# Causal attention between two expert layers: all scores of a head pair in one run, per-head work of exp, cast and low part merged, routing moved into the context bank

## What is computed

```
x = x + 0.5 * ffn(layernorm(x))      # 8 experts, the best one per token
x = x + attn(layernorm(x))
x = x + 0.5 * ffn(layernorm(x))
attn: q, k, v = tanh(x @ W + b)      # 16 heads of 64, per batch row of 512 tokens
      p = softmax(causal(q k^T / 8)); ctx = p v;  tanh(ctx @ Wo + bo)
ffn:  logits = x @ gate; e = argmax; first 320 tokens of an expert are kept
      relu(x @ w1[e] + b1) @ w2[e] + b2, times the probability of e
```

## Time and profile before

| | us |
|---|---|
| median of 3 runs | 523.68 (523.2 to 523.76) |
| profiled execution | 527.28 |
| its span, first to last instruction | 525.5 |
| TensorE busy | 434.2 (83%) |
| VectorE busy | 304.7 (58%) |
| ScalarE busy | 254.5 (48%) |
| POOL busy | 255.6 (49%) |
| mean granted TensorE clock | 0.929 of full |

### The profile page before, as it was taken

The page is one execution under the profiler, slowest core; times in us unless marked ns, Lnnn a source line. Parts: engine busy times, 40 slices in busy tenths (PEclk is TensorE's granted clock), DMA queues, the critical chain, the costliest instruction groups (busy, mean ns, idle before and its releaser), DMA issues.

```text
span 525.5 us, 11791 instructions
## 1 busy us (share of the span) xinstructions
PE 434.2 (83%) x4395; PEld 294.2 (56%) x4395; DVE 304.7 (58%) x926; ACT 254.5 (48%) x441; POOL 255.6 (49%) x277
## 2 busy tenths in 40 slices
PE   1742999528799999999999999899999788499960
PEld 1611687404566766566576566566666543167850
DVE  6781344638977767378856488774698713222213
ACT  1100433106587888487757577775777511034310
POOL 6471154712765565265455556456556440205550
PEclk9995899958899999999989999999999887789995
DMA  8812343163000000000000000000000000125315
GB/s 269 288 53 53 95 152 100 51 221 128 1 2 1 2 2 2 0 2 2 1 2 1 23 2 1 3 1 11 13 1 2 2 20 1 45 73 161 123 54 167
DMA packets 31515, 28.06 MB, mean 53 GB/s; under 512 B 2732, under 2 KB 27365, under 8 KB 31208
## 3 DMA queue, kind: packets, MB, share of 16 engines
q1 hardware_dynamic: 27184, 19.97, 12.7%
q0 software_dynamic: 2560, 4.74, 2.8%
q10 hardware_dynamic: 1720, 2.66, 1.4%
HBM read 16.84 MB, written 10.52 MB: 52 GB/s over the span
## 4 chain that ended last, share of the span: by engine, by line
PE 61%; DVE 12%; POOL 10%; issue 9%; DMA 5%; ACT 1%; SPq 0%; DVEq 0%; POOLq 0%; ACTq 0%
PE sc L710 12%; PE sc L589 7%; PE pj L599 7%; PE pj L680 5%; PE tT L747 4%; PE cx L730 3%; PE cx L732 3%; PE sc L715 3%; PE pj L690 3%; DVE Ph L1073 3%; POOL disp L332 3%; PE cx L731 3%; PE tT L551 3%; DMA ytok<-empty 3%; POOL Pl L360 2%
## 5 line engine op out<-in xcount | busy, mean ns | idle before, releaser
L360 POOL TENSOR_TENSOR Pl<-Pf,Ph 128x512 f16<-128x512 f32 (+1 forms) x64 | 61.9, 982 | 74.6 <-DVE Ph L1073 74.6
L710 PE MATMUL sc<-Tq,Tk 64*128 64x128 f32 (+3 forms) x512 | 95.5, 471 | 0.0
L360 POOL TENSOR_TENSOR Pl<-Wf,Ph 128x512 f16<-128x512 f32 (+1 forms) x64 | 58.6, 931 | 49.2 <-DVE Ph L1073 49.2
L343 POOL DMA_INDIRECT ytok<-Y,who x48 | 49.5, 1031 | 67.8 <-DVE Y L941 56.7
L1073 DVE CAST Ph<-Pf 128x512 f16<-128x512 f32 (+1 forms) x96 | 55.2, 607 | 41.6 <-ACT Pf L494 40.9
L730 PE MATMUL cx<-Vh,Ph 128*128 128x65 f16 x640 | 66.7, 197 | 14.1 <-POOL Vl L360 10.6
L434 ACT ACTIVATE hT<-sc,RT 128x320 f32<-128x320 f32 x64 | 33.8, 528 | 91.2 <-PE sc L589 90.3
L730 PEld LDWEIGHTS cx<-Vh,Ph 128*128 128x128 f16 x640 | 59.8, 99 | 16.4 <-POOL Vl L360 12.0
L731 PE MATMUL cx<-Vl,Ph 128*128 128x64 f16 x640 | 66.7, 195 | 0.0
L732 PE MATMUL cx<-Vh,Pl 128*128 128x65 f16 x640 | 66.5, 195 | 0.0
L1073 DVE CAST Ph<-Wf 128x512 f16<-128x512 f32 (+1 forms) x96 | 53.8, 591 | 20.0 <-ACT Wf L494 19.6
(11 more groups left out here) (181 smaller groups left out, 876.3 us busy)
## 6 DMA issues: line engine op xcount, KB each, us to landing
W<-in_L_ffn_w SPq DMA_DIRECT2D x32, 256.0 KB
disp<-empty SPq DMA_DIRECT2D x2, 1290.0 KB, 7.4
XE<-disp SPq DMA_DIRECT2D x16, 129.0 KB
ytok<-empty SPq DMA_DIRECT2D x2, 1024.0 KB, 12.6
G<-ytok SPq DMA_DIRECT2D x8, 256.0 KB, 3.8
out<-X SPq DMA_DIRECT2D x4, 256.0 KB, 2.3
ytok<-Y,who POOLq DMA_INDIRECT x48
XE<-disp SPq DMA_DIRECT2D x16, 32.2 KB
```

The lines of the kernel that those rows point to most:

```text
L343: pool.indirect_dma_start(ytok[phase], bass.IndirectOffsetOnAxis(ap=who[u][0:m, j:j + 1], axis=0), Y[u][0:m, j, :], None).then_inc(y_sc[u] ...
L360: pool.tensor_tensor(dst, src, hi, ALU.subtract).then_inc(done, 1)
L710: mm(score_bank(h, c)[:, o:o + w], Tk[u][half(h), P * kt:P * kt + P], Tq[u][half(h), P * kt:GN], start=kt == kts[0], stop=False)
```

## The change

- The two heads of a pair share tiles: Pf, Ph and Pl become [128, 2, 1280], and one exp, one cast and one low cover both heads of a chunk.
- TensorE does all scores of a pair in one run, then all masks, then the context of head 0. Chunk 2 of both heads goes to halves of bank pj1; the second half waits until the first is written (`half_ps`). Chunk c of head h is in sc[2c + h] otherwise.
- K is projected ahead of Q, and waits in pj1 for the exp of chunk 2 of the pair before. Tanh of K comes ahead of tanh of Q.
- ScalarE casts V (`v_high`) ahead of the exps, and all three exps come ahead of tanh of V.
- POOL does the low of V first, then one low of chunk 0 for both heads. VectorE does the lows of chunks 1 and 2, each behind its cast.
- A context waits for all lows of its pair at head 0.
- Routing goes into bank cx, in step 7 (logits) and in step 0 of the batch after (ranks), each right behind the projections and behind a wait for normalise of head 1 of pair i - 3. `choose` stays in step 7, `place` is now ahead of the first cast of step 0.
- The last output projection uses pj0.

```diff
-ORDER = [(c, h) for c in range(3) for h in range(2)]
-POOL_LOWS = [(0, 0), (0, 1), (2, 0), (2, 1)]
-V_LOWS = [(1, 0), (1, 1)]
+SCORED = [(c, h) for c in range(3) for h in range(2)]
+SCORES_IN = (2, 4, 6)
...
+        Pf0, Ph0 = sb("Pf0", [P, 2, 1280], F32), sb("Ph0", [P, 2, 1280], F16)
+        Pf = [Pf0, Wf[:, 0:2560].rearrange("p (h n) -> p h n", h=2)]
+        Ph = [Ph0, sb("Ph1", [P, 2, 1280], F16)]
+        Pl = [sb(f"Pl{u}", [P, 2, 1280], F16) for u in range(2)]
...
-        sc = [bank(f"sc{i}") for i in range(4)]
+        SC = ctx.enter_context(nc.psum_tensor("sc", [P, 4, 512], F32))
+        sc = [SC[:, i, :] for i in range(4)]
...
+        def scored(s, u, c):
+            a, n, _ = CHUNKS[c]
+            source = pj1[:].rearrange("p (h n) -> p h n", h=2) if c == 2 else SC[:, 2 * c:2 * c + 2, :]
+            return slice(a, a + n), source, 6 * s + SCORES_IN[c]
 
         def score_bank(h, c):
-            return sc[2 * h + (c == 1)]
+            return pj1[:, 256 * h:256 * h + 256] if c == 2 else sc[2 * c + h]
...
             def p_low(s, u):
-                for c, h in POOL_LOWS:
-                    a, n, _ = CHUNKS[c]
-                    pool.wait_ge(S["p_hi"], 6 * s + 2 * c + h + 1)
-                    low(Pl[u][h][:, a:a + n], Pf[u][h][:, a:a + n], Ph[u][h][:, a:a + n], S["p_lo_p"])
+                pool.wait_ge(S["p_hi"], 3 * s + 1)
+                low(Pl[u][:, :, 0:GN], Pf[u][:, :, 0:GN], Ph[u][:, :, 0:GN], S["p_lo_p"])
...
                 if score:
+                    v_low(i - 1, 1 - u)
                     p_low(i - 1, 1 - u)
-                    v_low(i - 1, 1 - u)
...
             def exps(s, u, c):
-                a, n, _ = CHUNKS[c]
-                for h in range(2):
-                    act.wait_ge(S["s_ps"], 6 * s + 2 * c + h + 1)
-                    if not (isinstance(s, int) and s < 2):
-                        act.wait_ge(*low_part(s - 2, h, c))
-                    act.activation(Pf[u][h][:, a:a + n], score_bank(h, c)[:, 0:n], ACT.Exp, scale=0.125,
-                                   bias=pshift[:]).then_inc(S["exp_done"], 1)
+                at, source, ready = scored(s, u, c)
+                act.wait_ge(S["s_ps"], ready)
+                if s >= 2:
+                    act.wait_ge(*((S["p_lo_v"], 2 * (s - 2) + c) if c else (S["p_lo_p"], s - 1)))
+                act.activation(Pf[u][:, :, at], source, ACT.Exp, scale=0.125, bias=pshift[:]).then_inc(S["exp_done"], 1)
...
                 if score:
-                    exps(i - 1, 1 - u, 0)
-                    exps(i - 1, 1 - u, 1)
+                    v_high(i - 1, 1 - u)
+                    for c in range(3):
+                        exps(i - 1, 1 - u, c)
                 if project:
                     tanh_v(i, u)
-                if score:
-                    exps(i - 1, 1 - u, 2)
                 if turn:
                     copy_ct(i - 3, (r - 3) % NPAIR)
-                if score:
-                    v_high(i - 1, 1 - u)
...
-                if not first:
-                    pe.wait_ge(S["tv"], i)
-                for w, ps, done in ((0, pj0, "q_ps"), (1, pj1, "k_ps")):
-                    if w and not first:
-                        pe.wait_ge(S["tk"], i)
-                    if w and r == 0 and not first:
-                        pe.wait_ge(S["rank_read"], NS + b - 1)
+                for w, ps, done in ((1, pj1, "k_ps"), (0, pj0, "q_ps")):
+                    if w and i == 1:
+                        pe.wait_ge(S["tk"], 1)
+                    if w and i >= 2:
+                        pe.wait_ge(S["exp_done"], 3 * (i - 2) + 3)
+                    if not w and i:
+                        pe.wait_ge(S["tv"], i)
...
+            def scores(s, u, project):
+                if s:
+                    pe.wait_ge(S["exp_done"], 3 * s)
+                pe.wait_ge(S["tq"], s + 1)
+                pe.wait_ge(S["tk"], s + 1)
+                def part(h, c, kt):
+                    o, q = KOFF[kt] - CHUNKS[c][0], P * kt
+                    return mm(score_bank(h, c)[:, o:o + GN - q], Tk[u][half(h), q:q + P], Tq[u][half(h), q:GN],
+                              start=(c, kt) in ((0, 0), (1, 1)) or (c, h) == (2, 0), stop=False)
                 for h in range(2):
+                    part(h, 0, 0)
+                for h in range(2):
+                    part(h, 1, 1)
+                for h in range(2):
+                    part(h, 1, 3)
+                if project:
+                    pe.wait_ge(S["tk"], s + 2)
+                part(0, 2, 2).then_inc(S["half_ps"], 1)
+                pe.wait_ge(S["half_ps"], s + 1)
+                part(1, 2, 2)
+                for c, h in SCORED:
...
             def context(c, u, h):
                 if h == 0:
                     pe.wait_ge(S["v_lo"], c + 1)
-                pe.wait_ge(S["p_hi"], 6 * c + h + 5)
-                pe.wait_ge(*low_part(c, h, 2))
-                pe.wait_ge(*low_part(c, h, 1))
-                if h or not (isinstance(c, int) and c == 0):
+                    pe.wait_ge(S["p_lo_p"], c + 1)
+                    pe.wait_ge(S["p_lo_v"], 2 * c + 2)
+                if c or h:
                     pe.wait_ge(S["ctxn"], 2 * c + h)
...
                 if project:
-                    qk(i, b, r)
+                    kq(i, b, r)
+                if route:
+                    pe.wait_ge(S["ctxn"], 2 * (i - 3) + 2)
+                    route()
                 if early:
                     if turn:
                         tt_free(i - 3)
                     early()
                 if score:
-                    scores(i - 1, 1 - u, 0)
-                    scores(i - 1, 1 - u, 1, c1_read)
+                    scores(i - 1, 1 - u, project)
                 if mix:
+                    if cx_read:
+                        pe.wait_ge(*cx_read)
                     context(i - 2, u, 0)
                 if project:
                     v(i, b, r)
-                if score:
-                    scores(i - 1, 1 - u, 2)
...
-                late = {7: lambda: rank_batch(b - 1, pj1)}
-                end = {6: lambda: route_logits(b - 1, sc[1])}
-                c1_read = {7: (S["dl_ready"], NS + b)}
+                route, cx_read = {7: lambda: route_logits(b - 1, cx)}, {7: (S["dl_ready"], NS + b)}
+                if b > 1:
+                    route[0], cx_read[0] = lambda: rank_batch(b - 2, cx), (S["rank_read"], NS + b - 1)
...
+            step(NG, 0, project=False, route=lambda: rank_batch(NG - 2, cx), cx_read=(S["rank_read"], NS + NG - 1))
...
+            def p_high(s, u, c):
+                at = scored(s, u, c)[0]
+                dve.wait_ge(S["exp_done"], 3 * s + c + 1)
+                if s >= 2:
+                    dve.wait_ge(S["ctx_ps"], 2 * (s - 2) + 2)
+                dve.tensor_copy(Ph[u][:, :, at], Pf[u][:, :, at]).then_inc(S["p_hi"], 1)
...
                 if score:
-                    split_high(i - 1, 1 - u, 0)
+                    p_high(i - 1, 1 - u, 0)
                 if mix:
                     normalise(i - 2, u, 0)
                 if score:
-                    split_high(i - 1, 1 - u, 1)
-                if late:
-                    late()
-                if score:
-                    split_low(i - 1, 1 - u)
-                    split_high(i - 1, 1 - u, 2)
+                    for c in (1, 2):
+                        p_high(i - 1, 1 - u, c)
+                        p_low(i - 1, 1 - u, c)
...
-                    step(b, r, between={4: lambda: add_out(b - 1), 5: lambda: norm_batch(b, b - 1),
-                                        7: lambda: choose(s, NS + b - 1, 0, GT, sc[1])}.get(r),
-                         late=(lambda: batch_place(b - 1, s, pj1)) if r == 7 else None)
+                    between = {4: lambda: add_out(b - 1), 5: lambda: norm_batch(b, b - 1),
+                               7: lambda: choose(s, NS + b - 1, 0, GT, cx)}
+                    if b > 1:
+                        between[0] = lambda: batch_place(b - 2, s, cx)
+                    step(b, r, between=between.get(r))
...
+            step(NG, 0, between=lambda: batch_place(NG - 2, s, cx))

```

More of the change, by code:

```diff
@@ L507, in step @@
                 if project:
-                    tanh_qk(i, r)
+                    tanh_kq(i, r)
                 if between:
@@ L692, in v @@
                 last.then_inc(S["v_ps"], 1)
-            def scores(s, u, c, bank_read=None):
-                first = isinstance(s, int) and s == 0
-                if c == 0:
-                    pe.wait_ge(S["tq"], s + 1)
-                    pe.wait_ge(S["tk"], s + 1)
-                if c == 2:
-                    pe.wait_ge(S["exp_done"], 6 * s + 2)
-                elif not first:
-                    pe.wait_ge(S["exp_done"], 6 * (s - 1) + (6 if c == 0 else 4))
-                if bank_read:
-                    pe.wait_ge(*bank_read)
-                a, n, kts = CHUNKS[c]
-                for kt in kts:
-                    o, w = KOFF[kt] - a, GN - P * kt
-                    for h in range(2):
```

(24 more changed lines are left out.)

67 lines of the change are left out of this document (21 added, 46 removed).

## The result

| | us |
|---|---|
| median before | 523.72 (523.2 to 525.42, 4 runs) |
| median after | 560.62 (558.53 to 564.24, 4 runs) |
| ratio | 1.0707 (1.0665 to 1.0749) |
| profiled execution after (before) | 558.53 (527.28) |

A forecast was written before the change was run, and what follows sets the result against it. TensorE's own list was taken to bound plain steps, with stalls for VectorE's lows elsewhere. Step terms of +23.2 and +4.5 for the clock gave +27.7 on 523.68: 551.4 us, range 531 to 562.

The forecast's parts named there:

- The plain step: Attention step without routing or rescaling: would grow from 7.98 to 8.3 us, +0.35 with roundings, in 28 steps.
- TensorE's list: TensorE's own work in a plain step: -0.62 for masks, +0.43 and +0.31 for chunk 2, sum +0.12 us.
- a passage: TensorE's switch from 128 rows to 64 and back around masks: costs 0.31 us, one in place of three.
- Rival 3: Merged cast over two heads loses its fast form and takes 1.226, +0.5 us a plain step: 565 us; chance 0.04.
- The chain on VectorE: Cast of chunk 1 waits for POOL's low (2.15); late normalise makes TensorE wait 2.6 us at logits and ranks.
- Rival 1: POOL's long instruction doesn't hold VectorE's cast, normalise ends 1.5 us earlier: 539.4, or 533 without plain stall; chance 0.22.
- Step 5: Rescaling step: later pow and normalise raise the second context's stall from 0.5 to 2.9 us; step some 10.9.
- steps 4 to 6: These steps of each batch together: +1.8 us, three times 5.4.
- The merged exps: ScalarE's merged exps save 3 x 0.2 us of its time, costed at nothing because ScalarE is busy 48%.
- First four steps, bound by VectorE: Start of the attention: VectorE gains lows and a v_low collision, loses some collisions; +1 us (-1 to +3).
- The clock: Granted clock halves behind long stalls: three more falls of 1.5 us for five new stalls, +4.5 (0 to +9).
- steps 7 and 0: Routing steps, logits then ranks: 23.0 us together against 19.6 and 18.1, +3.4 and +4.9, with 2.6 waits.

The follow-up runs named there:

- Experiment 3: The changed kernel with chunk 2 of the first head issued right behind chunk 0, chunk 2 of the second behind its own chunk 1: 542.33 us (ratio 1.0369).
- experiment 4: The changed kernel with the masks of each chunk right behind its scores again: 545.0 us (ratio 1.0411).
- experiment 2: The changed kernel with POOL's one low of 1024 columns as two of 512, one for each head: 559.58 us (ratio 1.067).
- Experiment 10: The changed kernel with one exp for each head again, six in place of three, casts and lows left merged: 565.14 us (ratio 1.0789).
- experiment 5: The changed kernel with normalise of the first head ahead of the cast of chunk 0 on VectorE: 568.69 us (ratio 1.0864).
- experiment 6: The changed kernel with POOL's low of V behind its low of chunk 0 again: 566.21 us (ratio 1.0805).

## Why the prediction was right, and where it was off

**The plain step** (8.3, measured 8.26) is right in each term: TensorE's list +0.13 for +0.12, the wait of the second context 0.15 for 0.2. Experiment 3 shows that the losses it named are the heads sharing a bank and the wait between the halves, and experiment 4 the 0.31 of a passage. Rival 3 is out: the merged cast took 0.69 (196.31), and the merged exp 1.11.

**The chain on VectorE** was forecast as POOL's low 2.15 (2.14), the cast behind it, normalise at T + 7.15 (7.18), and a wait for cx of 2.6 (2.64, 2.63, 2.64). Rival 1 rested on a cast that isn't held. The rule behind the forecast, that a cast ends just behind POOL's instruction, came from one row, and it held; on so thin a base that was in part luck. The Trainium skill (SBUF — State Buffer, Who interferes with whom) says that a VectorE instruction in a 2-port mode, or one with two SBUF inputs beside a GpSimd instruction that reads SBUF, contends with GpSimd, and that the first to issue keeps the shared interfaces for its whole length. The runs agree for both kinds: a cast of 2.23, subtractions of 2.06, 2.02 and 3.03. For this chain the forecast used only the first kind (the second only for a small product in step 5). By the second, splitting POOL's low hands the wait to the subtraction behind the cast, as experiment 2 shows.

**Step 5** (10.9) measured 10.95 in batches 2 and 3 and 11.32 in batch 1. In batch 2 it grew by 2.46. The waits of over 0.1 ahead of its two contexts grew by 2.14 (2.04 + 0.46, against 0.36 before); the rest is near the plain step's 0.28. The forecast had 2.4 for the stall. Its sum for steps 4 to 6 (+1.8, measured 1.75 in batches 2 and 3) leaves out the plain step's 0.35 in one of the three steps, and a stall taken somewhat too long makes up for that.

**"The merged exps ... I cost that at nothing"** has no effect on the sum, because the plain stall was computed with the exp of 1.11, but as a price it is wrong. Experiment 10 measured 0.15 a plain step. ScalarE's share (48% before) says nothing about it: the first exp lies on the path masks, exp, cast, normalise, second context. The forecast had written that path down and then judged the merge by the share.

**"First four steps, bound by VectorE: +1 (-1 to +3)"** is the term that failed, at +5.0 in the profiled execution. Three things were left out. Projection of K into pj1 waits for the exp of chunk 2 of the pair before, and in step 2, with no contexts yet to cover it, that is the 1.56 at 133.64. The second context's wait for normalise, which in a plain step is 0.15, stands here behind the rescaling and a product of 128x4 elements that met the low of V and took 1.07 in place of 0.16 (4.32, where TensorE had waited 2.85 before, for the low of V). And the granted clock was 0.50 behind it, in 145.30 to 147.00, and already in 123 to 126, where the kernel before had 0.90.

How large the term is changes with the execution and with small edits. In experiment 2's kernel, whose edit acts only from the end of the second step on, the first two take 12.8, with 1.00 in 124 to 128; in the change they take 14.2, with 0.68. So some 1.4 of the 5.0 go with a clock that differs between executions and not with the change. In experiment 10's kernel the wait of 4.32 is 2.53, the granted clock behind it is 1.00 (143.7 to 150), and the four steps take 34.5 against 37.9, only 1.6 more than before the change. Why its wait is shorter was not followed up.

**The clock** (three falls of 1.5) was short. Behind the new waits for cx it fell in the first step 7 and in the second step 0, in step 5 of batch 1, in the first four steps and in the last step. Two steps 7 with the same wait took 14.92 with a fall and 11.95 without: 3.0. The step 0 with a fall took 12.99; the other took 10.09 with 1.22 less of wait, which leaves 1.7 (12.99 - 10.09 - 1.22). Steps 5 and 6 of batch 1 are 1.6 longer than in the others. So steps 7 and 0 cost 12.3, of which the forecast had 8.3 and at least part of 4.5. Why a wait of 2.63 is followed by full clock at 349.43 and at 434.43, and one of 2.64 is not at 264.37 and 361.39, stays open. That the total came out within 3.5 of the forecast owes something to luck, as the clock and the start could have fallen either way.

## What to carry to other kernels

An order that saves the busiest engine's time by making its products later can be paid for on every engine behind it: work out when the last buffer of that chain comes free, and who now waits there. If work is moved to another bank, the price is the time at which that bank's reader is done, not the work's own length; here one `normalise` moved up gave back 20 us. And whether a shorter instruction pays is told by the path it lies on, not by its engine's busy share.

## What the runs showed of the hardware

VectorE and POOL excluded each other for whole instructions in more forms than the cast of the earlier trace rows: subtractions of two SBUF tiles took 2.02 to 3.03 for 1.23 alone (experiments 2, 5 and 6) and 1.49 for 0.69 (experiment 5), and a product of 128x4 elements took 1.07 for 0.16 (the change, at 141.50). The ends tell how: casts of 0.69 end 0.55 behind POOL's instruction (199.77 against 199.22), subtractions of 1.23 end 1.08 behind it (198.93 against 197.85 in experiment 2, 199.62 against 198.54 in 5), so each did all but some 0.15 of its work only once POOL's was over. POOL paid too: in experiment 6 its low of V took 1.57 in place of 1.12. In experiments 2, 5 and 6 whichever of these VectorE instructions came next was the one held, so splitting or reordering moved the delay and did not remove it. The other surprise is the size of a fall of the clock: 1.6 to 3.0 us, after waits of which others of the same length were followed by full clock.
